# Ten column widths instead of three for the Up products of a mixture-of-experts chunk

## What is computed

```python
logits = x @ Wg.T                                   # N = 4096 tokens, E = 8 experts
top_v, top_i = jax.lax.top_k(logits, K)             # K = 2
gates = jax.nn.softmax(top_v, axis=-1)
cap = int(N * K * CF / E)                           # 1280
exp_batches = jnp.zeros((E, cap, d)).at[flat_e, pos_safe].set(x[tok], mode='drop')
h = jnp.einsum('ecd,edf->ecf', exp_batches, W1)     # 512 -> 2 * 1024, "Up"
inp, gate = jnp.split(h, 2, axis=-1)
h = jax.nn.gelu(inp, approximate=False) * gate
exp_out = jnp.einsum('eci,eid->ecd', h, W2)         # 1024 -> 512, "Down"
```

## Time and profile before

| | |
|---|---|
| median of three executions | 1484.09 us |
| span of the profiled execution | 1484.9 us |
| TensorE busy | 1437.8 us |
| VectorE, ScalarE, GpSimd busy | 654.8, 592.8, 377.3 us |
| DMA, mean over the span | 91 GB/s |

### The profile page before, as it was taken

How to read it: one execution, slowest core, us unless ns; L and a number is a source line. 1 busy time by engine, 2 the same in 40 slices (tenths; PEclk the granted TensorE clock), 3 DMA queues, 4 the chain that set the end, 5 groups by cost and what they waited for, 6 DMA issues and landing times.

```text
span 1484.9 us, 22294 instructions
## 1 busy us (share of the span) xinstructions
PE 1437.8 (97%) x7508; PEld 1214.8 (82%) x7509; DVE 654.8 (44%) x1451; ACT 592.8 (40%) x1018; POOL 377.3 (25%) x366
## 2 busy tenths in 40 slices
PE   6999999989989989999999999999999999999997
PEld 5768887777876888888889888899889888898886
DVE  7535666567886663112533521165323321253111
ACT  5534554257776553212533421255323421253212
POOL 4202232137765412102103111021202112021111
PEclk9999999999997999999999999999999999999999
DMA  9410221218648764112524422155514422052112
GB/s 205 64 58 29 85 89 54 85 50 196 178 120 213 178 179 114 23 21 47 149 73 99 120 71 35 14 158 182 116 32 106 106 64 42 7 148 57 21 36 28
DMA packets 80678, 135.62 MB, mean 91 GB/s; under 512 B 31058, under 2 KB 31186, under 8 KB 79604
## 3 DMA queue, kind: packets, MB, share of 16 engines
q1 hardware_dynamic: 63252, 97.66, 24.1%
q0 software_dynamic: 17376, 37.30, 13.5%
HBM read 94.41 MB, written 40.53 MB: 91 GB/s over the span
## 4 chain that ended last, share of the span: by engine, by line
PE 88%; DVE 4%; ACT 2%; DMA 2%; issue 2%; POOL 1%; SPq 0%; POOLq 0%; DVEq 0%; ACTq 0%
PE pg L1049 16%; PE pg L1050 16%; PE pg L1051 16%; PE pj L1049 10%; PE pj L1050 10%; PE pj L1051 10%; PE pg L1316 2%; PE pj L1288 2%; PE pt L1456 2%; PE pg L1254 2%; PE pt L1070 1%; PE pt L1275 1%; DMA out_rows<-ost,etab 1%; PE pt L1200 1%; DMA slot_table<-pack,dest 1%
## 5 line engine op out<-in xcount | busy, mean ns | idle before, releaser
L1049 PE MATMUL pg<-xe_hi,w_hi 128*128 128x512 f32 (+2 forms) x1152 | 402.1, 349 | 3.8 <-DVE xe_lo L1532 2.9
L1050 PE MATMUL pg<-xe_lo,w_hi 128*128 128x512 f32 (+2 forms) x1152 | 401.6, 349 | 0.0
L1051 PE MATMUL pg<-xe_hi,w_lo 128*128 128x512 f32 (+2 forms) x1152 | 401.5, 349 | 0.0
L1998 DVE TENSOR_TENSOR hp<-gl,pg 128x512 f32<-128x512 f32 x136 | 93.6, 688 | 571.0 <-ACT gl L1020 550.6
L731 POOL DMA_INDIRECT out_rows<-ost,etab x62 | 99.3, 1601 | 723.8 <-ACT ost L1004 357.3
L1020 ACT ACTIVATE gl<-pg 128x512 f32<-128x512 f32 x136 | 81.4, 598 | 411.7 <-PE pg L1051 403.7
L1049 PEld LDWEIGHTS pg<-xe_hi,w_hi 128*128 128x128 f32 x1152 | 219.1, 190 | 29.4 <-issue 3.1
L1050 PEld LDWEIGHTS pg<-xe_lo,w_hi 128*128 128x128 f32 x1152 | 219.1, 190 | 24.9
L1051 PEld LDWEIGHTS pg<-xe_hi,w_lo 128*128 128x128 f32 x1152 | 219.1, 190 | 25.0
L1049 PE MATMUL pj<-w_hi,hg_hi 128*128 128x512 f32 x448 | 177.8, 397 | 0.0
L1050 PE MATMUL pj<-w_lo,hg_hi 128*128 128x512 f32 x448 | 175.2, 391 | 0.0
(11 more groups left out here) (260 smaller groups left out, 2014.8 us busy)
## 6 DMA issues: line engine op xcount, KB each, us to landing
stage<-w SPq DMA_DIRECT2D x96, 512.0 KB
xr<-x SPq DMA_DIRECT2D x8, 1024.0 KB, 8.8
out_rows<-xr SPq DMA_DIRECT2D x8, 1024.0 KB
x_rows<-xn SPq DMA_DIRECT2D x8, 1024.0 KB
x_in<-x SPq DMA_DIRECT2D x7, 1024.0 KB, 5.1
x_rows<-zrow POOLq DMA_DIRECT2D x1, 2304.0 KB, 8.5
late_xT<-xT_hi SPq DMA_DIRECT2D x2, 1024.0 KB, 3.8
late_xT<-xT_lo SPq DMA_DIRECT2D x2, 1024.0 KB, 5.9
```

What stands on the lines that cost most here:

```text
L1049: nc.tensor.matmul(o, lh, rh, start=start, stop=False)
L1050: nc.tensor.matmul(o, lh, rl, start=False, stop=False)
L1051: return nc.tensor.matmul(o, ll, rh, start=False, stop=stop)
L1998: v.tensor_tensor(hp[j % 2][:], gl[j % 2][:], pg[:, 2 + j % 2, :], ALU.mult).then_inc(s_hp, 1)
```

## The change

The list `UP_WIDTHS` holds ten widths, 224 to 512 in steps of 32. The function `up` takes a number of columns instead of a number of tiles. A recursive function halves the list and writes a tree of `If` and `Else`, in whose leaves stand ten copies of `up`; at run time the smallest width that is not below `left` is taken. Semaphores, the Down products and the other engines are unchanged.

```diff
@@ -42,6 +42,7 @@
+UP_WIDTHS = list(range(7 * GT // 16, GT + 1, GT // 16))
@@ -1433,9 +1434,8 @@
-                    def up(tiles):
-
-                        w = tiles * P
+                    def up(w):
+
                         pe.wait_ge(s_xelo, following)
                         for j in range(FJ):
                             pe.wait_ge(s_w_lo, e * WP + j + 1)
@@ -1474,13 +1474,18 @@
-                    with pe.If(left < 2 * P + 1):
-                        up(2)
-                    with pe.Else():
-                        with pe.If(left > 3 * P):
-                            up(4)
+                    def up_narrowest(widths):
+
+                        if len(widths) == 1:
+                            up(widths[0])
+                            return
+                        half = (len(widths) + 1) // 2
+                        with pe.If(left < widths[half - 1] + 1):
+                            up_narrowest(widths[:half])
                         with pe.Else():
-                            up(3)
+                            up_narrowest(widths[half:])
+
+                    up_narrowest(UP_WIDTHS)
```

## The result

The changed kernel takes 1688.62 us (median; 1674.79 to 1699.64) against 1485.98 for the kernel before on the same chip: a ratio of 1.136, 95% interval 1.132 to 1.140, or 203 us more. The forecast was +161 and the range +46 to +281, so sign, range and mechanism held, and the size was a fifth too small.

A forecast was written before the change was run, and what follows sets the result against it. TensorE, busy 97% of the span with an unbroken matmul stream, bounds the kernel. Slow instruction jumps and clock loss add 167 us, narrower columns save 6: 1484.1 + 161 = 1645 us, range 1530 to 1765.

The forecast's parts named there:

- The ring: TensorE's instruction store: 8 places; fetch-ahead goes after the current block, jump target after the last fetched; 37 jumps not held.
- ten 512-column chunks: Idle ahead of their Up products plus clock loss: six at 15.4 us, three at 11.9, one at 3.5.
- the one into 35: Jump into block 35, start of the 512 copy, only just asked for: 4.1 us, an estimate.
- 3 x 3.5 + 4.1 + 0.4 - 2.1 = 12.9: Idle per full 512-column chain: three slow jumps, the jump into 35, two tests, less the sequencer's 2.1 us lead.
- (d): Rival: serial fetches, a slow jump waiting for the fetch ahead, 4 us more each; 1765 us and up; chance 0.08.
- The clock: After long idle ahead of a 512-column chunk, TensorE's lowered clock costs 2.5 us more.
- A lone slow head: A chunk whose only slow jump is to the loop's head block: 3.5 + 0.4 - 2.1 + 1.7 = 3.5 us.
- The narrow products: Up matmuls at 224 columns: 0.107 to 0.117 us apart, taken as 0.109, saving 6 us over three chunks.
- (a): Rival: the store holds all that four widths touch, only the 6 us gain shows, 1478 us; chance 0.06.
- (b): Rival: large store where only first visits to blocks stall, 1485 to 1500 us; chance 0.06.
- (c): Rival: store of 12 places, 13 slow jumps, 1540 us; chance 0.08 with its surroundings, 1500 to 1560.
- (e): Rival: narrow matmul pairs are no closer, 0.12 us; 6 us on any case; no chance given.

The follow-up runs named there:

- the dead copy: Kernel before plus a fourth Up copy inside the loop, between the choice and the tail, never run and jumped over by a test: 1.0389, 58 us more.
- four copies: Changed kernel with only the widths 224, 256, 384 and 512, the ones this input uses: 1.0212, 31 us more than the kernel before.
- four copies with 512 first: Changed kernel with widths 224, 256, 384, 512 only, the 512 copy placed first behind the first test: 1.0077, 11 us more than before.
- the 9-block loop: Kernel before plus a 224-column width; 224 and 256 copies hold steps 0 to 4, share 5 to 7; no never-run code ahead: 1.0093, +14 us.

## Why the prediction was right, and where its sizes were off

**The cause: right, and shown.** Code inside the loop and not widths, tests or the program's size: the four kernels with one of these alone measure -7.7 (narrower columns), -2 (tests), 0 (size) and +58 us (code in the loop). The marks that the prediction named are all there: 131 instruction packets in the loop for "some 120", branches of 3.0 to 7.0 us, 10 us and more of idle ahead of all ten 512-column chunks, the fallen clock behind it and unchanged spacing further inside.

**The number of places: supported.** The model was that the store has 8 places of 16 KB. The cliff between 8 and 9 blocks (+1 and +14 us with the same loop) is where it says, if blocks are counted as the model counts them, with the one fetched ahead. The Trainium skill (Runtime: NRT & Kernel Launch, Instruction fetch mechanics) gives 128 KiB in blocks of 16 KiB, which is 8 too; the two agree.

**The rule of replacement: only roughly right.** The ring reproduces the kernel before exactly and the changed one approximately: its 37 jumps to blocks not held and the 9 into a block only just asked for are 46, measured 53. It has some 60 for the dead copy (measured 29), 36 for four copies (18), 16 for four copies with 512 first (10), and 15 or more were expected of the 9-block loop (13). So the number was nearly right where everything is thrashed, and up to double where the loop is only one or two blocks too long. What the real rule is stays open; the traces show which jumps are slow, and not what stood in which place.

**The forecast's sum, term by term,** in us. Measured is idle ahead of the chunk beyond the usual 0.2 us, and what the first matmuls lose at the lower clock, read off the spacing; for 384 columns also 1.2 us behind a slow jump to the tail.

| term | forecast | measured |
|---|---|---|
| ten 512-column chunks | 92 + 36 + 3.5 = 131.5 | 173 |
| two of 256 | 14 | 16.5 |
| two of 384 | 13 | 19 |
| three of 224 | 8.5 | 2 |
| end of the loop | 0 | 4 |
| fewer columns | -6 | -4.5 |
| sum | +161 | +210 |

The span grew by 209.0.

- *How many chunks have the whole chain, mis-sized; the largest part of the error, some 27 of 49 us.* The model had six 512-column chunks with three jumps before the one into 35, three with two of them (36 us) and one with the head alone (3.5). In the trace nine have all four, and one, the first, three. A chunk with all four costs 17.7 us in the mean, so the three cost 53, and the one costs 14. This is the replacement rule again: the block of the head is gone each time.
- *Chained jumps, mis-sized; some 14 us more, six chunks at 17.7 instead of 15.4.* The step was "3 x 3.5 + 4.1 + 0.4 - 2.1 = 12.9", and two errors in it partly cancel. In the nine full chains the four jumps took 4.0, 4.9, 5.4 and 3.6 us in the mean, 17.9 together, where the prediction has 3.7 three times and 4.1; the sequencer's lead was 3.6 to 3.9 us instead of 2.1. In the gap shown above, from 763.4 to 782.9 are 19.5 us, less 3.7 is 15.8.
- *What makes a slow jump dearer.* Of the 53, 25 have one instruction packet starting in them and took 3.0 to 4.9 us, mean 3.6; 27 have two and took 4.3 to 6.0, mean 5.1. The instruction queue during the lone jump at 848.9 us (3.4 us; 848.9 to 852.2), then during the one at 763.4 (4.6 us; 763.4 to 768.0):

```profile
q8 instruction: 1, 0.02, 1.9%
...
q8 instruction: 2, 0.03, 4.7%
```

  In the nine chains of four the second and third jump have two, and the last, into a block already asked for, has one. The loop's branch, which comes first, has two in the four chains behind a chunk of at most 256 columns (4.6 to 4.9 us) and one in the others. That fits a fetch ahead, begun at or before the jump, that stands in its way. It is what rival (d) held, at about 1.4 us a jump instead of 4. This reading is argued from durations and counts: no run took the fetch ahead away.
- *The clock: right.* 2.5 us were taken for a long gap; the ten chunks lost 1.6 to 3.0. All chunks together lost some 33 us. After a gap of 1 us none was lost.
- *A lone slow head: too dear.* "3.5 + 0.4 - 2.1 + 1.7" took 2.1 us of lead, read at the first wait of the Up copy. But the slow jump is the loop's branch, and that comes earlier, ahead of the head and the tests. In the same chunk of the kernel before it ran at 559.0, 3.2 us ahead of the matmul at 562.14:

```profile
L1428 PEldq COMPARE_BRANCH  x1: 77/77/77, 559.0 to 559.0; - x1
```

  In the changed kernel it is 3.6 to 3.9 us ahead of the end of the last matmul, and in four copies 2.6 of 3.4 us are covered. Hence 1 us for each of two chunks, none for the third, and no loss of clock. The lead was read at the wrong instruction.
- *The end of the loop: left out.* After the last chunk the sequencer goes through the rounds that have nothing to do. The loop's branch takes 3.6 us once more, and the next one 6970 ns, with three instruction packets starting in it:

```profile
L1428 PEldq COMPARE_BRANCH  x24: 76/3494/6970, 556.5 to 1693.6; - x24
```

  From the start of the last matmul to the end of the span are 12.5 us, 8.4 before: 4.1 us that no term of the sum had.
- *The narrow products: right within bounds.* First and last of the 192 in the 207-token chunk:

```profile
853.56 0.36 PE L1050 MATMUL pg<-xe_hi,w_hi 128*128 128x224 f32 x1 [0.80 <-issue]
...
874.98 0.28 PE L1052 MATMUL pg<-xe_hi,w_lo 128*128 128x224 f32 x1
```

  21.42/191 = 0.1121 us apart, inside the 0.107 to 0.117 that was given and above the 0.109 taken. A chunk saves 22.91 - 21.42 = 1.5 us, three save 4.5.

**The rivals.** (a), that the store holds all that is touched, falls with the 131 packets. (b), first visits only, falls too: the last 512-column chunk still waits for the whole chain. (c), 12 places, falls with the cliff at 9 blocks. (d) was too large in size; its kind fits the jumps with two packets, but isn't shown. (e) falls with the 0.1121.

What stays open: the rule of replacement, and with it a way to say beforehand whether a loop of 9 or 10 blocks costs 11 us or 58; what in a fetch ahead makes a jump dearer; and whether a version with the full gain of the narrowing and no loss exists. One with all 8 steps at 224 columns needs a fourth copy, and no loop of at most 8 blocks was built with four.

## What to carry to other kernels

Specialised copies inside a loop are paid in instruction blocks of 256. Count the loop's instructions on TensorE (the other engines were not tried): while they and the block behind them fit in 8 blocks, copies, tests and skipped code had no cost that these runs can tell. Past that, what counts is how many blocks not held the most frequent path jumps through in a row: put its copy behind the first test (24 us instead of 203 for the same ten copies), before thinking of fewer copies. No version with the 224-column copy beside the others beat the three copies of before: the narrowing is worth 4.5 us, and the best loop of more than 8 blocks still took 11 us more than before. In the profile the sign is "issue" ahead of an engine that used to be full, together with packets on its instruction queue late in the kernel; that queue silent through the loop is the sign of the opposite.

## What had not been expected of the hardware

- One block decides, and so does where the loop begins: 97 instructions that never run, ahead of the loop, took 1.0093 to 1.0005, and the slow jumps from 13 to 1.
- Code that is only jumped over costs too: 400 such instructions in the loop were +58 us, while 2,800 ahead of it were +0.1 (interval -2.4 to +2.8).
- A slow jump is dearer when two instruction packets start in it: 4.3 to 6.0 us, mean 5.1, against 3.0 to 4.9, mean 3.6, with one (52 jumps of the changed kernel).
- At 224 columns a matmul with its own weight load is 0.1121 us behind the one before. The line through 256 and 512 columns, on which 384 lies too (33.14/191 = 0.1735, the chunk at 1122.08 us of the kernel before), says 0.1066, so it ends between 256 and 224 columns.
